# Routed feed-forward on one core: the sorted tokens in eight tiles of 512 and one of 256, placed on the chip, in place of nine tiles of 512

## The reference

```python
x = _layernorm(x + attn(x))
xf = x.reshape(-1, 256)                       # 4096 tokens
top1 = argmax(softmax(xf @ gate_w.T))         # 2 experts
masked = xf[None] * one_hot(top1).T[:, :, None]
h = relu(einsum('end,edh->enh', masked, w1) + b1[:, None])   # hidden: 1024
routing = (einsum('enh,ehd->end', h, w2) + b2[:, None]).sum(0)
shared = relu(xf @ sw1 + sb1) @ sw2 + sb2
out = _layernorm(x + (routing + shared).reshape(x.shape))
```

## Time and profile before

| | |
|---|---|
| median of 3 runs | 987.3 us (985.47 to 989.46) |
| the profiled execution's own time | 986.67 us |
| its span in the trace | 984.9 us |
| busy: PE, DVE, ACT, POOL | 85%, 56%, 58%, 26% of the span |
| mean granted clock of PE | 0.935 of full speed |
| token tiles (shared network) | 494 to 752 us |
| expert tiles | 752 to 968.7 us, then sums and scatters to 976.5 |

### The profile page before, as it was taken

One profiled execution on the slowest core, in us unless ns is written; L12 is line 12 of the kernel. 1 busy time (PEld: TensorE's weight loads), 2 busy tenths in 40 slices (PEclk: granted clock), 3 DMA queues, 4 the chain that ended last, 5 costly groups with the idle time before them and its releaser, 6 DMA issues. The chain is left out here.

```text
span 984.9 us, 18061 instructions
## 1 busy us (share of the span) xinstructions
PE 840.3 (85%) x6689; PEld 600.2 (61%) x6689; DVE 556.4 (56%) x1160; ACT 568.3 (58%) x733; POOL 252.7 (26%) x200
## 2 busy tenths in 40 slices
PE   7269926999998799999678899889996999999993
PEld 5157712343333333333367888779886999998993
DVE  3348864665765465566587756674552355445543
ACT  4247725888888688888634453453342445454451
POOL 4224431000100100020145452444142233333333
PEclk9679966999999799999989999999998999999997
DMA  7785557566856565593291111111036444443301
GB/s 154 91 295 189 177 128 134 114 112 107 125 97 111 93 114 96 100 136 54 52 248 55 55 55 55 44 50 60 22 142 227 158 163 151 151 151 132 127 23 43
DMA packets 61806, 112.96 MB, mean 115 GB/s; under 512 B 9412, under 2 KB 50409, under 8 KB 56297
## 3 DMA queue, kind: packets, MB, share of 16 engines
q1 hardware_dynamic: 56824, 99.07, 43.2%
q0 software_dynamic: 4896, 12.73, 3.5%
HBM read 58.15 MB, written 30.82 MB: 90 GB/s over the span
## 5 line engine op out<-in xcount | busy, mean ns | idle before, releaser
L873 ACT ACTIVATE probs<-slots 128x1024 f32<-128x1024 f32 x288 | 275.0, 1031 | 49.2 <-DVE slots L942 39.9
L942 DVE TENSOR_TENSOR slots<-slots,bias_t 128x512 f32<-128x512 f32 (+1 forms) x288 | 159.2, 604 | 77.8 <-PE slots L975 75.9
L1644 DVE TENSOR_TENSOR h_lo<-h_f,h_hi 128x512 fp32r<-128x512 f32 x136 | 104.6, 771 | 129.7 <-PE o_ps L1742 78.8
L993 PE MATMUL o_ps<-probs,v_st 128*32 128x256 f32 (+1 forms) x2560 | 155.5, 365 | 0.8 <-ACT probs L873 0.8
L993 PEld LDWEIGHTS o_ps<-probs,v_st 128*32 128x32 f32 x2560 | 67.5, 110 | 77.8 <-issue 48.8
L975 PE MATMUL slots<-q_first,k_st 99*128 99x512 bf16 (+3 forms) x384 | 83.5, 343 | 31.6 <-DVE v_st L887 16.0
L1484 ACT ACTIVATE h_f<-slots,b_cur 128x512 f32<-128x512 f32 x72 | 49.5, 688 | 102.6 <-PE slots L1728 91.6
L1484 ACT ACTIVATE h_f<-slots,b_c 128x512 f32<-128x512 f32 x64 | 44.0, 687 | 95.6 <-PE slots L1728 94.0
L1488 ACT ACTIVATE h_hi<-h_f 128x512 fp32r<-128x512 f32 x136 | 86.0, 632 | 4.3
L975 PE MATMUL slots<-q_second,k_st 99*128 99x512 bf16 (+3 forms) x384 | 80.5, 329 | 7.7 <-ACT probs L873 7.7
L1045 POOL TENSOR_TENSOR y_t<-y_t,rs_row 128x2048 f32 (+1 forms) x4 | 18.2, 4562 | 258.5 <-DMA rs_row<-rsum_d 258.5
(11 more groups left out here) (207 smaller groups left out, 1889.8 us busy)
## 6 DMA issues: line engine op xcount, KB each, us to landing
qk_d<-parts SPq DMA_DIRECT2D x32, 384.0 KB, 2.6
cur_hi<-experts_hi SPq DMA_DIRECT2D x9, 1024.0 KB, 4.8
cur_lo<-experts_lo SPq DMA_DIRECT2D x9, 1024.0 KB, 7.2
k_st<-qk_d SPq DMA_DIRECT2D x16, 384.0 KB
q_first<-qk_d SPq DMA_DIRECT2D x48, 128.0 KB
q_second<-qk_d SPq DMA_DIRECT2D x48, 128.0 KB
xs_sb<-xs_d SPq DMA_DIRECT2D x9, 528.0 KB, 5.1
bs_sb<-base_d SPq DMA_DIRECT2D x9, 512.0 KB, 4.0
```

The lines of the kernel that those rows point to most:

```text
L873: nc.scalar.activation(probs[:, k % PBUFS, :, 0:w], slots[:, k % SLOTS, :, 0:w], ACT.Exp).then_inc(exped, 1)
L942: ins = dve.tensor_tensor(tile, tile, bias_t[:, h0:h0 + 2, first:first + w], ALU.add)
L993: ins = pe.matmul(o_ps[32 * j2:32 * j2 + 2 * D, half, q:q + w], v_st[:, g, j, j2, :], probs[:, (k + j2 // 2) % PBUFS, j2 % 2, col:col + w] ...
L1644: dve.tensor_tensor(h_lo[:, n % 3], h_f[:, q % 2], h_hi[:, n % 3].bitcast(F32), ALU.subtract).then_inc(hl_ok, 1)
```

## The change

The expert tiles are no longer nine aligned tiles of 512 rows. There are eight of 512, and a last one (u = 16) of 256, `blocks(u)` being 4 or 2. Expert 0 gets as many full tiles as its number of tokens holds 512s, rounded to the nearest; expert 1 gets the others. One of the two then has up to 256 rows left over, and they make the half tile. So the first row of each tile depends on the data: DVE works out nine row numbers (`row_i`) and nine expert numbers (`expert_i`) behind `place(7)`. SP reads the row number into a register before each load of rows and of base rows. In the last tile every instruction of PE, ACT, DVE and POOL that runs over the tile's rows is cut to 256 of them, and two output scatters are left out of its four. The pad rows and the size of `xs_d` and `base_d` are as before.

```diff
-        nc.scalar.activation(xt_hi, two_banks, ACT.Copy).then_inc(xh_ok, 1)
+        w = P * blocks
+        nc.scalar.activation(xt_hi[:, :, 0:w], two_banks[:, :, 0:w], ACT.Copy).then_inc(xh_ok, 1)
...
+    def blocks(u):
+        return NB if u < LAST_U else NB // 2
...
+            def rows_of(j):
+                return sp.value_load(row_i[0:1, j:j + 1], min_val=0, max_val=SLOTS_D - P * blocks(FIRST + j))
+
             def load_rows(j):
-                src = xs_d[TT * j:TT * j + TT].rearrange("(k p) c -> p k c", p=P)
-                sp.dma_start(xs_sb[j % 2][:, :, :], src).then_inc(xs_ld[j % 2], 16)
+                nk = blocks(FIRST + j)
+                src = xs_d[bass.ds(rows_of(j), P * nk)].rearrange("(k p) c -> p k c", p=P)
+                sp.dma_start(xs_sb[j % 2][:, 0:nk, :], src).then_inc(xs_ld[j % 2], 16)
...
-            sp.wait_ge(route_ok, 2)
+            sp.wait_ge(route_ok, 3)
...
-            sp.wait_ge(out_done, 16 * NB * EXP_TILES)
+            sp.wait_ge(out_done, 16 * (NB * TILES + blocks(LAST_U)))
...
-            pool.iota(tile_start[:, :], pattern=[[TT, EXP_TILES]], base=0, channel_multiplier=0,
+            pool.iota(tile_start[:, :], pattern=[[TT, TILES]], base=TT // 2, channel_multiplier=0,
...
             def put_out(j):
 
-                for k in range(NB):
+                for k in range(blocks(FIRST + j)):
...
-                    dve.tensor_scalar(expert_i[:, :], tile_start[:, :], n_first[:, 0:1], None, ALU.is_ge).then_inc(route_ok, 1)
+
+                    halved = second[:, TILES:EXP_TILES]
+                    dve.tensor_scalar(second[:, 0:TILES], tile_start[:, :], n_first[:, 0:1], None, ALU.is_gt).then_inc(first_ok, 1)
+                    dve.wait_ge(first_ok, 3)
+                    dve.tensor_reduce(full[:, 0:1], second[:, 0:TILES], AX.X, ALU.add).then_inc(first_ok, 1)
+                    dve.wait_ge(first_ok, 4)
+                    dve.tensor_scalar(full[:, 1:2], full[:, 0:1], -float(TT), float(TT * TILES), ALU.mult, ALU.add
+                                      ).then_inc(first_ok, 1)
+                    dve.wait_ge(first_ok, 5)
+                    dve.tensor_tensor(halved, full[:, 1:2], n_first[:, :], ALU.is_gt).then_inc(first_ok, 1)
+                    dve.scalar_tensor_tensor(row_f[:, 0:TILES], second[:, 0:TILES], float(TT), tile_start[:, :], ALU.mult, ALU.add
+                                             ).then_inc(first_ok, 1)
+                    dve.wait_ge(first_ok, 7)
+                    dve.tensor_scalar(row_f[:, 0:TILES], row_f[:, 0:TILES], -float(TT // 2), None, ALU.add).then_inc(first_ok, 1)
+                    dve.scalar_tensor_tensor(row_f[:, TILES:EXP_TILES], halved, float(TT // 2), full[:, 1:2], ALU.mult, ALU.add
+                                             ).then_inc(first_ok, 1)
+                    dve.wait_ge(first_ok, 9)
+                    dve.tensor_copy(row_i[:, :], row_f[:, :]).then_inc(route_ok, 1)
+                    dve.tensor_copy(expert_i[:, :], second[:, :]).then_inc(route_ok, 1)
...
-                for k in range(1, NB):
+                for k in range(1, blocks(LAST_U)):
                     sums(k)
                     scaled(k - 1)
-                scaled(NB - 1)
+                scaled(blocks(LAST_U) - 1)
...
-                        ins = pe.matmul(l1_bank[q % 2], w1_of(u, w)[:, kc, P * q:P * q + P],
-                                        (xt_hi, xt_lo)[a][:, kc, :],
+                        ins = pe.matmul(l1_bank[q % 2][:, 0:P * blocks(u)], w1_of(u, w)[:, kc, P * q:P * q + P],
+                                        (xt_hi, xt_lo)[a][:, kc, 0:P * blocks(u)],
...
-                for k in range(NB):
+                for k in range(blocks(u)):
                     if q == 0 and u:
```

More of the change, by code:

```diff
@@ L953, in _ @@
                 shared_low(0)
-                tile.low_x1(dve, 0)
+                tile.low_x1(dve, 0, NB)
             @block.tensor
@@ L1151, in norm1_end, with low_x1 @@
                               ).then_inc(x1_ok, 1)
-    def low_x1(dve, u):
+    def low_x1(dve, u, blocks):
+        w = P * blocks
         dve.wait_ge(xh_ok, u + 1)
-        dve.tensor_tensor(xt_lo, two_banks, xt_hi.bitcast(F32), ALU.subtract).then_inc(xl_ok, 1)
+        dve.tensor_tensor(xt_lo[:, :, 0:w], two_banks[:, :, 0:w], xt_hi[:, :, 0:w].bitcast(F32), ALU.subtract
+                          ).then_inc(xl_ok, 1)
     def project(pe, t):
@@ L1255, in feed_forward @@
     slot_i = sb("slot_i", [P, 2, NB], I32)
-    tile_start = sb("tile_start", [1, EXP_TILES]); n_first = sb("n_first", [1, 1])
+    tile_start = sb("tile_start", [1, TILES]); n_first = sb("n_first", [1, 1])
+    second = sb("second", [1, EXP_TILES]); row_f = sb("row_f", [1, EXP_TILES]); full = sb("full", [1, 2])
     n_first_i = sb("n_first_i", [1, 1], I32); expert_i = sb("expert_i", [1, EXP_TILES], I32)
+    row_i = sb("row_i", [1, EXP_TILES], I32)
     pad_row = sb("pad_row", [P, ROW])
@@ L1441, in put_out @@
                                             ).then_inc(out_done, 16)
-            pool.wait_ge(route_ok, 2)
+            pool.wait_ge(route_ok, 3)
             pool.wait_ge(const_ok, 1)
@@ L1483, in _ @@
                         act.wait_ge(hl_ok, n - 1)
-                    nc.scalar.activation(h_f[:, q % 2], l1_bank[q % 2], ACT.Relu, bias=bias).then_inc(hf_ok, 1)
+                    w = P * blocks(u)
+                    nc.scalar.activation(h_f[:, q % 2, 0:w], l1_bank[q % 2][:, 0:w], ACT.Relu, bias=bias).then_inc(hf_ok, 1)
                     act.wait_ge(hf_ok, n + 1)
@@ L1504, in _ @@
                 if u < LAST_U:
-                    tile.high_x1(act, u + 1)
-            for k in range(NB):
+                    tile.high_x1(act, u + 1, blocks(u + 1))
+            for k in range(blocks(LAST_U)):
                 root2_last(k)
@@ L1643, in _ @@
                         dve.wait_ge(l2_done, n - 2)
-                    dve.tensor_tensor(h_lo[:, n % 3], h_f[:, q % 2], h_hi[:, n % 3].bitcast(F32), ALU.subtract
+                    w = P * blocks(u)
+                    dve.tensor_tensor(h_lo[:, n % 3, 0:w], h_f[:, q % 2, 0:w], h_hi[:, n % 3, 0:w].bitcast(F32), ALU.subtract
                                       ).then_inc(hl_ok, 1)
@@ L1671, in _ @@
                 if u < LAST_U:
-                    tile.low_x1(dve, u + 1)
+                    tile.low_x1(dve, u + 1, blocks(u + 1))
                     gather(u)
@@ L1710, in turn_rows @@
                 if j == 0:
-                    pe.wait_ge(route_ok, 2)
+                    pe.wait_ge(route_ok, 3)
                 for kc in range(KC):
-                    for k in range(NB):
+                    for k in range(blocks(FIRST + j)):
                         ins = pe.transpose(slots[:, 1, kc, P * k:P * k + P], xs_sb[j % 2][:, k, P * kc:P * kc + P],
```

19 lines of the change are left out of this document (10 added, 9 removed).

## The result

The changed kernel takes 979.5 us (median of 6 runs, 976.2 to 980.9), the kernel before 988.05 (985.2 to 989.5): a ratio of 0.9925, interval 0.9908 to 0.9943. On a second chip, timed again, it is 0.9918 (0.9893 to 0.9943). The forecast was 980.8, or 6.5 us less than before; the two ratios stand for 7.4 and 8.1 us, the two differences of the medians are 8.6 and 6.4.

The account below looks back on a forecast made before the run. Expert tiles were taken as bound by PE matmul columns, the end by DVE's sums and POOL's scatters. Terms -0.4 - 4.4 - 2.9 + 1.2 = -6.5 us gave 980.2, with 0.6 for the median 980.8; range 976.5 to 985.8.

Parts of the forecast that it names:

- The last tile: Last expert tile: landing of the tile before's scatters, not PE, releases the last sums, at T0 (its first matmul) + 17.0.
- The term, 4.4 us: Last tile: sums start at T0 + 17.0 instead of T0 + 21.42, gaining 4.4 us; bounds 2.5 to 4.8.
- PE's own 11 us: Last tile: halved hidden and output matmuls take 8 x 1.37 = 11.0 us off PE, the naive gain.
- The rival's T0 + 10.6: Last tile: for PE to set the end, the fourth scatter would have to land before T0 + 10.6; chance 0.06.
- Two scatters less: After the last sums: two output scatters instead of four bring the last issue 2.9 us forward.
- The front: Before the expert tiles: nine small DVE operations delay SP's queue by 1.2 us, its register load hidden; bounds 0 to 2.6.
- One to one behind the turn: After PE's turn to the expert tiles: the front's 1.2 us delay passes on 1:1.
- The transposes left out: End of the tile before the last: four fewer transposes bring T0 0.43 us forward, counted as 0.4.
- The slower rival: Eight expert tiles: POOL takes DVE's port in each, costing 10 us, so 990.8; chance 0.08.
- PE as the end: Last tile: PE sets the end and scatters don't hold the sums; 11.0 us gained, so 974.2; chance 0.06.
- The sum: Whole kernel: -0.4 - 4.4 - 2.9 + 1.2 = -6.5 us, giving 980.8 as the median.

Follow-up runs that it names:

- e1: The changed kernel, but its last tile writes to its own buffer and the last sums no longer wait for the previous tile's scatters; 0.9893 of the kernel before.
- e2: The kernel before, with nine full tiles, plus an own output buffer for the last tile and no wait for the previous tile's scatters; 0.9992 of the kernel before.
- after_again: The changed kernel run once more, unaltered, on a second chip; 0.9918 of the kernel before.
- e3: The changed kernel's row numbers, register loads and nine operations, but nine full tiles with aligned rows; 1.0021 of the kernel before, 1.0015 when run again.
- e4: The changed kernel's half tile without the new front: aligned rows, old expert numbers, last 256 sorted rows left out; 0.9932 of the kernel before, 0.9909 again.
- e5: The changed kernel with pad writes released by the gap's position alone, and first weights by expert numbers computed ahead of the row numbers; 0.9920 of the kernel before.
- e6: The changed kernel with the first rows loaded ahead of the first weights; 0.9875 of the kernel before.
- e9: The kernel before, nine full tiles, with own last-tile buffer, first rows ahead of weights and first bias copied early; 0.9904 of the kernel before.

## Why the prediction was right

**The last tile: right, and larger than worked out.** The step was that the landing of tile 7's scatters, not PE, releases the last sums. The profile shows it by name, e1 removes it and gains 4.0 us, e2 removes it where it isn't binding and gains nothing. The term, 4.4 us, measured 5.4, which is outside the 2.5 to 4.8 that I gave it. Its parts: scaling of tile 7 done at T0 + 8.8 (9.3 expected; 954.28 + 1.39 - 946.85), first scatter 0.80 later (0.80), the fourth 4.09 after it (4.44), the sums 2.49 after that (2.5). ACT's halves at 470 and 419 ns were estimated at 500 and 430 from the 512 and 1024 wide ones. The scatters I took as fixed; they got shorter, by 0.35 us in all. Another 0.16 of the difference is the T0 of the kernel before: I counted from 946.39, the first matmul stands at 946.23.

**PE's own 11 us** did leave PE, less some waiting: its last matmul starts 12.1 us after T0 (958.95), about 12 expected, where it was 22.2. The rival's T0 + 10.6 took no such waiting into account. Even with the landing out of the way (e1) the sums come at 12.13, so 9.4 of the 11.0 us would reach them, not all.

**Two scatters less: right.** 3.0 us against 2.9.

**The front: its sum near the 1.2, but not by the path that I gave.** Nine operations put 1.14 us on DVE (1.2). The turn came 0.95 us later from the places. Over all executions with this front (after, after_again, e1, e3 twice) it comes at 19.0 to 19.5, without it (before, e2, e4 twice) at 17.9 to 18.5: 1.05 between the means. To the first relu it was 1.85, 0.74 on the second chip, 1.85 in e1, and 0.8 and 1.0 in e3: their mean is 1.3. The bounds, 0 and 2.6, held. In between, though, "whole" and "hidden" don't describe it. The first rows are issued 13.3 to 13.4 us behind the places, where without the new front it was 10.3 to 11.8: 2.35 later in the mean. SP's register load stands behind the landing of the row scatters and takes 0.85 us in after_again, not 0.27; with its register instructions the rows are issued 1.3 us after the load's start. What gives this back is the rows' own landing, 5.6 to 6.0 us against 6.0 to 7.6. I had left it at 7.2. So the +1.2 came out of 2.35 less 1.3, and that it met DVE's 1.1 is in part luck. How much of the 2.35 is the queue's start, how much POOL's slower scatter and how much the register load, no run parts (see e5).

**One to one behind the turn: not always.** Of the 1.85 us to the relu, 0.9 lies between the turn and the relu (13.05 against 12.15), in e1 1.0, in after_again and e3 0.1 or less. The table by stretches, of the 5 us from the turn on, first the changed kernel, then after_again:

```profile
746.10:751.10 5.00, 5.00 (x24) 5.00 (x25) 1.23 (x1) 1.03 (x1) 0.00 (x0) 0.50 0.89 324
750.02:755.02 5.00, 5.00 (x30) 5.00 (x31) 1.23 (x1) 1.02 (x1) 0.00 (x0) 0.66 0.94 343
```

The same time holds 24 matmuls at a granted clock of 0.50 (1.2 GHz) and 30 at 0.66. In the 2 us ahead of the turn, while PE stood still, the clock had already fallen in the changed kernel and e1 (0.60 and 0.68 in the mean), not in after_again and the kernel before (1.00). The prediction has no term for this. The idle time before the turn was 3.71 us, 4 expected, the turn itself at 746.1 in place of 748.0, since this execution reached the places 1.65 us earlier.

**The transposes left out**, 0.43 us, can't be seen: the distance from the first relu to T0 is 187.70 and 186.79 against 187.28, because other things in it vary by more.

**The slower rival didn't come.** POOL's addition met DVE's passes where it did before, and not in every tile. The timeline of DVE in the changed kernel, against the earlier trace rows:

```profile
901.92 3.32 DVE L1678 TENSOR_TENSOR h_lo<-h_f,h_hi 128x512 fp32r<-128x512 f32 x2 [1.39 <-ACT h_hi L1503]
```

That is 3.32 us for two passes, 0.69 longer than before. The answer for the tile `h_lo`, of the same 190 us (its passes, ns as min/median/max):

```profile
L1678 DVE TENSOR_TENSOR h_lo<-h_f,h_hi x66: 424/693/2718, 760.5 to 949.6; 128x512 fp32r<-128x512 f32 x64, 128x256 fp32r<-128x256 f32 x2
```

Half of the passes take 693 ns or less. Besides the two above, one other takes over 1 us (2.52 at 768.07), and the same one took 2.32 in the kernel before; the rest are below 0.97. PE as the end is out: the sums start at T0 + 16.20, and 4.1 us earlier when only PE and its chain hold them (e1).

**The sum.** -6.5 forecast. By rows from the places to the last issue the two profiled executions of the changed kernel are 6.1 and 8.1 us shorter than before's; by time 8.6 between the medians, 7.4 by the ratio of the first measurement. The 1 us or so between forecast and measurement is the size of the 5.4 for 4.4; that nothing else shows is partly luck, for the stretch from the first relu to T0 alone varies by up to 1.7 us between executions that do the same there.

## What to carry to other kernels

When a loop's last step gets cheaper on the engine that bounds it, look at every wait that the step after it has beside that engine: here one output buffer and one counter released the sums 0.4 us before PE did, and took back 4.0 of 9.4 us as soon as PE got faster (21.56 less 12.13 with the wait removed, against 5.4 with it). A price for the step is then the distance to the second release, worked out from rows, and not the work removed. And small operations ahead of a semaphore that starts a transfer queue aren't free, though the engine that runs them has time to spare: here 1.14 us of them, with a register load and a slower scatter beside them, made the turn 1.05 us later.

## What the runs showed that I had not expected

A scatter on POOL takes longer when it is issued while an h_lo pass runs on DVE, and the longer the more of the pass is left. With passes of 512 columns tile 7's first scatter took 1.37 us (pass at 960.33, scatter at 960.53) and with passes of 256 it took 1.12 (956.27, 956.47); scatters issued with no pass running take 0.97 to 1.00 in the expert tiles. In the two kernels, scatters issued with 0.23, 0.32 and 0.49 us of a pass left took 1.08, 1.18 and 1.37. In the changed kernel the second row scatter at the front, with 1.17 us of two passes left, took 2.01 us:

```profile
727.26 0.96 POOL L1421 DMA_INDIRECT xs_d<-x,slot_i  x1 [8.56 <-DVE slot_i L1567]
728.52 2.01 POOL L1421 DMA_INDIRECT xs_d<-x,slot_i  x1 [0.30 <-issue]
730.83 0.96 POOL L1421 DMA_INDIRECT xs_d<-x,slot_i  x1 [0.30 <-issue]
```

It is issued at 728.52, and a pair of passes had begun at 728.42. In e5, where the pair starts behind the scatter's issue, all four take 0.96 to 0.97. One row stands apart: in the kernel before, the first of these scatters took 1.53 us (728.91) with a pair begun 0.02 us after it. The coincidence holds in each of these runs; the cause was not tried by itself. The Trainium skill (SBUF — State Buffer, Who interferes with whom) infers that descriptor generation doesn't wait for a two-input operation such as this one; these rows speak against that.

Row scatters land late behind other transfers. In e6 the last one, beside the 1 MB of pad writes issued 1.3 us later than in the kernel before, took 5.4 us to land, against 2.4 for output scatters at the end. The answer for its line, of e6:

```profile
DMA to landing us min/median/max: 5.4/5.4/5.4
```

In e9, whose pads start 1.3 us earlier, SP could issue the first rows 7.75 us behind the places, in e6 11.62; 0.8 of this lies between the start of e6's register load and the issue.
